# Who empties the turned keys: ScalarE alone with two buffers, or ScalarE and VectorE with three

## The reference, cut to what matters

```python
kv = (cond @ Wkv + bkv).reshape(1, -1, 2, H, hd)
k, v = (kv[:, :, 0], kv[:, :, 1])
q = _fq_sym(q, axis=-1)      # per head: max|x|/127, round, scale back
k = _fq_sym(k, axis=-1)
v = _fq_sym(v, axis=2)       # one scale per channel over all 4096 rows
attn = jnp.einsum('bhqd,bhkd->bhqk', q, k)
```

## Time and profile before

| what | value |
|---|---|
| time, median of 3 runs | 683.85 us (683.26 to 685.11) |
| the profiled execution | 682.87 us, span 681.1 us |
| granted TensorE clock, mean | 0.92 |
| `kv_stage`, first to last instruction | about 281.0 to 350.2 us |
| PE, DVE, ACT, POOL busy over the span | 86%, 72%, 59%, 49% |

### The profile page before, as it was taken

How to read it: one execution, slowest core, us unless ns; L and a number is a source line. 1 busy time by engine, 2 the same in 40 slices (tenths; PEclk the granted TensorE clock), 3 DMA queues, 4 the chain that set the end, 5 groups by cost and what they waited for, 6 DMA issues and landing times. The chain is left out here.

```text
span 681.1 us, 12859 instructions
## 1 busy us (share of the span) xinstructions
PE 587.4 (86%) x4813; PEld 398.3 (58%) x4813; DVE 493.7 (72%) x846; ACT 401.7 (59%) x754; POOL 335.9 (49%) x265
## 2 busy tenths in 40 slices
PE   4976899997899999788964988988888878889997
PEld 3542354444677776567740565655555465668886
DVE  4357999996677874567776999999999955433322
ACT  4226975552535544457875999999999953421111
POOL 1009999996204443243615889888888840000000
PEclk9987999999999999999975787779879869999999
DMA  8626600000936664035566889896979738900000
GB/s 336 254 74 252 247 0 1 0 1 0 303 119 212 211 218 130 16 115 147 150 167 149 162 129 183 152 168 136 165 159 149 132 64 326 408 2 1 0 1 15
DMA packets 97091, 92.90 MB, mean 136 GB/s; under 512 B 70596, under 2 KB 88324, under 8 KB 93639
## 3 DMA queue, kind: packets, MB, share of 16 engines
q1 hardware_dynamic: 84352, 85.74, 46.3%
q10 hardware_dynamic: 12678, 6.36, 3.2%
HBM read 68.59 MB, written 6.62 MB: 110 GB/s over the span
## 5 line engine op out<-in xcount | busy, mean ns | idle before, releaser
L2133 DVE TENSOR_REDUCE d_nmax<-d_psum 128x1 f32<-128x1024 f32 x128 | 152.0, 1214 | 6.0 <-PE d_psum L2289 6.0
L2289 PE MATMUL d_psum<-kst,qT 96*128 96x512 bf16 x256 | 97.2, 479 | 32.8 <-ACT d_e L2230 13.6
L528 POOL TENSOR_TENSOR b_h<-b_h,b_cb 128x1024 f32<-128x1024 f32 x32 | 88.0, 2750 | 6.5 <-DVE b_h L578 5.7
L2230 ACT ACTIVATE d_e<-d_psum,d_nmax 128x1024 f32<-128x1024 f32 x64 | 71.3, 1118 | 14.5 <-DVE d_nmax L2133 14.0
L2113 POOL TENSOR_SCALAR d_rounded<-d_e,d_lift 128x1024 f16<-128x1024 f32 x64 | 72.8, 1137 | 13.0 <-issue 7.0
L2113 POOL TENSOR_SCALAR d_rounded<-spare,d_lift 128x1024 f16<-128x1024 f32 x62 | 70.2, 1133 | 16.9 <-ACT d_lift L2234 12.6
L578 DVE TENSOR_TENSOR_SCAN b_h<-b_dA,b_psum 128x1024 f32<-128x1024 f32 x32 | 73.1, 2286 | 2.5 <-ACT b_dA L633 2.0
L633 ACT ACTIVATE b_dA<-b_dtT,b_A 128x248 f32<-128x248 f32 x128 | 53.7, 490 | 33.1 <-DVE b_h L578 28.1
L2230 ACT ACTIVATE spare<-d_psum,d_nmax 128x1024 f32<-128x1024 f32 x64 | 71.4, 1121 | 1.9 <-DVE d_nmax L2133 1.9
L2316 PEld LDWEIGHTS d_psum<-d_ident_f,d_rounded 128*128 128x128 f16 x512 | 44.1, 120 | 32.8 <-issue 20.9
L689 PE MATMUL b_psum<-b_bdiag,b_dtx 128*128 128x512 f32 x128 | 60.2, 594 | 0.8 <-DVE b_h L578 0.8
(11 more groups left out here) (439 smaller groups left out, 1185.5 us busy)
## 6 DMA issues: line engine op xcount, KB each, us to landing
c_w<-in_w0gu SPq DMA_DIRECT2D x16, 768.0 KB, 4.8
kst<-kT_scratch SPq DMA_DIRECT2D x84, 128.0 KB, 2.7
w<-in_w SPq DMA_DIRECT2D x5, 1920.0 KB, 21.0
b_cb<-c_scratch SPq DMA_DIRECT2D x4, 2048.0 KB, 6.9
c_w<-in_w0dn SPq DMA_DIRECT2D x16, 384.0 KB, 5.7
kT_scratch<-k_kT ACTq DMA_DIRECT2D x15, 384.0 KB, 2.7
a_ctx<-in_ctx SPq DMA_DIRECT2D x2, 2048.0 KB, 19.8
k_ctxT<-in_ctxT SPq DMA_DIRECT2D x12, 256.0 KB, 3.0
```

The costliest lines, as they stand in the source:

```text
L528: nc.gpsimd.tensor_tensor(hv, hv, cv, ALU.mult).then_inc(hc_ready, 1)
L2133: nc.vector.tensor_reduce(nm[:, t, m:m + 1, f:f + 1], quarter(m, j).unsqueeze(1), AX.X, ALU.max, negate=True).then_inc(nm_ready, 1)
L2230: nc.scalar.activation(e[j].unsqueeze(1), quarter(m, j).unsqueeze(1), ACT.Exp, bias=nm[:, t, m:m + 1, f], accum_out=zp[:, t, m:m + 1, f]). ...
L2289: last = nc.tensor.matmul(quarter(m, j)[:, b * 512:(b + 1) * 512], qT[0:QROWS, m:m + 1, t * P:(t + 1) * P], kst[m % 2][0:QROWS, at:at + 51 ...
```

## The change

ScalarE keeps the first turned step of each iteration and now copies it at the head of its iteration, ahead of `copy_values` and `split0`. VectorE copies the second turned step of the iterations that have two (steps 2, 4, 7, 9), directly behind `quantize_keys`, and steps 14 and 15 as before. There are three alternating `kT` buffers and the one for the last step. The stores of steps 0 to 11 are issued by SyncE between its context loads, those of steps 12 to 15 by ScalarE. Two semaphores, one for each copying engine, replace `kT_ready`. The maxima of the values are cut otherwise: iteration 4 takes 2 steps, 7 takes 3, and 8, 9 and 10 take 1 each (before: iterations 3, 5, 7 and 9, 2 steps each).

```diff
-VALUES_MAX = {3: (5, 7), 5: (7, 9), 7: (9, 11), 9: (11, 13)}
+VALUES_MAX = {4: (5, 7), 7: (7, 10), 8: (10, 11), 9: (11, 12), 10: (12, 13)}
+BY_VECTOR = tuple(turned[1] for turned in TURNS if len(turned) == 2) + (14, 15)
+BY_SCALAR = tuple(m for m in range(16) if m not in BY_VECTOR)
+KT_SLOTS = 3
...
-        kT = [sb(f"k_kT{s}", [P, K_PARTS * KC, KEYS], BF16) for s in range(2)] + [g["kT_last"]]
+        kT = [sb(f"k_kT{s}", [P, K_PARTS * KC, KEYS], BF16) for s in range(KT_SLOTS)] + [g["kT_last"]]
...
+        def wait_copied(eng, m):
+
+            copied, own = (kT_by_vector, BY_VECTOR) if m in BY_VECTOR else (kT_by_scalar, BY_SCALAR)
+            eng.wait_ge(copied, own.index(m) + 1)
+
+        def store(queue, m):
+            wait_copied(queue, m)
+            queue.dma_start(g["kT_store"][:, :, m * KEYS:(m + 1) * KEYS], kT[slot(m)][:, :, :]).then_inc(kT_stored[slot(m)], 16)
+
+        def wait_slot(eng, m):
+
+            if KT_SLOTS <= m < LAST:
+                eng.wait_ge(kT_stored[m % KT_SLOTS], m // KT_SLOTS * 16)
...
-                for m in range(FIRST + CTX_SLOTS - 1, STEPS):
-                    if m >= FIRST + CTX_SLOTS:
-                        sp.wait_ge(v_psum, nth(m - CTX_SLOTS))
-                    load_context(sp, d, g, m)
-                for s in range(2):
-                    sp.wait_ge(kT_stored[s], EARLY_STEPS // 2 * 16)
+                for i in range(STEPS - FIRST):
+                    m = FIRST + CTX_SLOTS - 1 + i
+                    if m < STEPS:
+                        if i:
+                            sp.wait_ge(v_psum, i)
+                        load_context(sp, d, g, m)
+                    for turned in TURNS[i]:
+                        if turned < EARLY_STEPS:
+                            store(sp, turned)
+                for s in range(KT_SLOTS):
+                    sp.wait_ge(kT_stored[s], EARLY_STEPS // KT_SLOTS * 16)
...
                     quantize_keys(FIRST + i)
+                    for m in TURNS[i][1:]:
+                        copy_turned(m)
                     queries(i)
...
                 for i in range(STEPS - FIRST):
+                    for m in TURNS[i][0:1]:
+                        copy_turned(m)
                     if i:
                         copy_values(FIRST + i - 1)
                     split0(FIRST + i)
-                    for m in TURNS[i][0:1]:
-                        copy_turned(m)
                     split1(FIRST + i)
-                    for m in TURNS[i][1:]:
-                        copy_turned(m)
                     for m in TURNS[i]:
-                        store(m)
+                        if m >= EARLY_STEPS:
+                            store(act, m)
...
                     if m >= 2:
-                        pe.wait_ge(kT_ready, m - 1)
+                        wait_copied(pe, m - 2)
```

More of the change, by code:

```diff
@@ L1524, in layer1_memory @@
     g["qs"] = sb("qs", [P, TC, H, 100], BF16)
-    g["kT_stored"] = [sem(f"kT_stored{s}") for s in range(3)]
+    g["kT_stored"] = [sem(f"kT_stored{s}") for s in range(KT_SLOTS + 1)]
     g["w_inT"] = sb("w_inT", [P, KC, 2 * INNER])
@@ L1674, in kv_stage @@
         kT_psum = sem("k_kT_psum")
-        kT_ready = sem("k_kT_ready")
+        kT_by_scalar = sem("k_kT_by_scalar")
+        kT_by_vector = sem("k_kT_by_vector")
         kT_stored = g["kT_stored"]
@@ L1687, in slot @@
         def slot(m):
-            return 2 if m == LAST else m % 2
+            return KT_SLOTS if m == LAST else m % KT_SLOTS
+        def wait_copied(eng, m):
[7 more added lines that the diff above has]
+                eng.wait_ge(kT_stored[m % KT_SLOTS], m // KT_SLOTS * 16)
         psT = [ps[:, 4 + 2 * s:6 + 2 * s, :].rearrange("p a b -> p (a b)").bitcast(BF16)[:, 0:K_PARTS * KC * KEYS]
@@ L1769, in copy_turned @@
                     dve.wait_ge(kT_psum, m + 1)
[L1770 to L1773, removed]
+                    wait_slot(dve, m)
+                    nc.vector.tensor_copy(kT[slot(m)][:, :, :], psT[m % 2]).then_inc(kT_by_vector, 1)
                 for i in range(STEPS - FIRST):
@@ L1824, in copy_turned @@
                     act.wait_ge(kT_psum, m + 1)
[L1825 to L1831, removed]
+                    wait_slot(act, m)
+                    nc.scalar.activation(kT[slot(m)][:, :, :], psT[m % 2], ACT.Copy).then_inc(kT_by_scalar, 1)
                 def split0(m):
@@ L1875, in _ @@
                 keep_queries(0)
-                store(LAST - 1)
+                store(act, LAST - 1)
                 keep_queries(1)
-                store(LAST)
+                store(act, LAST)
                 act.wait_ge(v_copied, nth(LAST))
@@ L2055, in _ @@
                 last_keys(sp, g["kT_last"], kst[0], k_in[0], 0, range(TAKEN, len(PRODUCTS)))
-                sp.wait_ge(g["kT_stored"][0], STEPS // 2 * 16)
-                sp.wait_ge(g["kT_stored"][1], (STEPS // 2 - 1) * 16)
+                for s in range(KT_SLOTS):
+                    sp.wait_ge(g["kT_stored"][s], STEPS // KT_SLOTS * 16)
                 load_keys(sp, d, kst[0], k_in[0], 0, LATE, range(TAKEN, len(PRODUCTS)))
@@ L2060, in _ @@
                 last_keys(sp, g["kT_last"], kst[1], k_in[1], 1)
-                sp.wait_ge(g["kT_stored"][2], 16)
+                sp.wait_ge(g["kT_stored"][KT_SLOTS], 16)
                 for dst, name in ((wp, "wp"), (bp, "bp")):
@@ L2214, in _ @@
                 last_keys(act, g["kT_last"], kst[0], k_in[0], 0, range(TAKEN))
-                act.wait_ge(g["kT_stored"][0], STEPS // 2 * 16)
-                act.wait_ge(g["kT_stored"][1], (STEPS // 2 - 1) * 16)
+                for s in range(KT_SLOTS):
+                    act.wait_ge(g["kT_stored"][s], STEPS // KT_SLOTS * 16)
                 load_keys(act, d, kst[0], k_in[0], 0, LATE, range(TAKEN))
```

## The result

Twelve runs of the changed kernel have a median of 682.57 us, twelve of the kernel before 684.48; the ratio is 0.9946, with a 95% interval of 0.992 to 0.9973. In microseconds of 683.85 that is 3.7 won, interval 1.8 to 5.5, where 3.0 were forecast (680.85, range 679.0 to 682.7; 683.85 x 0.9946 = 680.2). A second measurement of the same kernel on the chip of the last experiments gave 0.9958, interval 0.9931 to 0.9984.

What follows compares the result with a forecast made beforehand. TensorE, stalled by ScalarE's copies, was taken to bind before, ScalarE from iteration 5 on after. Gain: 2.7 us at step 10, 0.0 beyond, 0.3 credit, 3.0 in all: 683.85 to 680.85 us, range 679.0 to 682.7.

Steps and rivals of the forecast that it cites:

- TensorE unhindered through iteration 5: TensorE's 5.3 us of waits for ScalarE's copies gone through iteration 5; iteration 6 starts near 311.5.
- The bound was ScalarE from iteration 5 on: Steps 10 to 15: ScalarE's five rounds, uncovered while GpSimd works, take 26.8 us where TensorE would want 24.5.
- `split0` of step 15 carries the end: Stage end: a fixed chain of 6.19 us follows this `split0`, so the stage gains only what step 15 gains there.
- 2.7 us won at step 10: Iteration 5: VectorE has step 10 quantized at 313.0, where `split0` of step 10 started at 315.71 before.
- Nothing won from step 10 to step 15, 27.8 against 27.9: ScalarE's rounds 26.8, plus 0.4 for GpSimd's query rest and 0.6 for shared-access holds: 27.8 us, against 27.9 traced.
- 0.3 credited for my walk's own error: The walk put through the kernel before ended 0.7 us later than the trace; half, 0.3, was added to the gain.
- Stores and third buffer at nothing: Stores moved to SyncE, third key buffer: both priced 0, as a store's issue holds ScalarE for nothing; stores' other bound 4.4 us.
- Copies not held by GpSimd: VectorE's four new copies from PSUM: taken as 0 held; copies as slow as 1.4 us would cost 2.3.
- Rival 2: VectorE late in iterations 4 to 6 by slow copies or held quantization: 2.3 of 3.0 us go, 683.1; chance 0.12.
- rival 1: ScalarE does not bind because its rounds are shorter: the whole 6.4 us stall goes, 677.5; chance 0.06.
- rival 3: VectorE's thicker work holds GpSimd in ScalarE's uncovered rounds: slower, 686 at 0.6 a piece, 689.6 at the extreme; chance 0.06.
- Rival 4: The gain does not pass the barrier; the next stage's opening, with late keys, takes it back: 683.9; chance 0.06.

Runs made afterwards that it cites:

- the last experiments: Changed kernel with ScalarE's copy under the GpSimd round in iteration 10, or iterations 7 to 10, and VectorE's last two maxima moved: ratios to before 0.9921 and 0.9943.
- experiment 5: Changed kernel with ScalarE's first query part done twice in iteration 5 (2.03 us put in): stage 68.37 us against 65.93, 2.44 longer.
- experiments 1: Changed kernel with ScalarE making all copies, the second of an iteration behind `split1`, VectorE only steps 14 and 15: stage 72.70 us against 65.93.

## Why the prediction was right, step by step

- **TensorE unhindered through iteration 5.** Right, nearly to the digit: iteration 6 was forecast at 311.5 and starts at 313.02, which by before's start of the stage (1.52 earlier) is 311.50.
- **The bound was ScalarE from iteration 5 on.** Right: behind `split0` of step 10 its row has no gap but the rounds' waits for GpSimd, and experiment 5 gives back all of what it adds. That `split0` of step 15 carries the end was right too: 6.19 us behind it before, 6.22 after.
- **2.7 us won at step 10.** Too high: 34.54 - 32.57 = 1.97. VectorE quantized step 10 at 313.0 in my sum; by the same start it was 313.7. I had 0.3 for what GpSimd holds up; the trace has this:

```profile
311.00 1.16 POOL L1827 TENSOR_TENSOR k_parts<-k_rest,k_parts 128x512 bf16<-128x512 f32 x1 [0.74 <-ACT k_parts L1859]
...
311.08 1.36 DVE L1788 TENSOR_TENSOR v_own_max<-v_own_max,k_v_step_max 128x256 f32<-128x256 f32 x1
```

  GpSimd started 0.08 us ahead, and the 0.43 addition took 1.36, the same 0.93 as in the earlier trace rows.
- **Nothing won from step 10 to step 15, 27.8 against 27.9.** It took 27.14, so 0.8 were won. The five rounds by the rows were 26.8; of the 1.0 that I added, 0.3 came in sum. The 0.4 for GpSimd's rest of the queries was right (0.17 and 0.33 beyond 1.27). The 0.6 for holds did not come, and the third query part, which is shorter, took 1.53 where I had 1.78. The sum at step 15 is 2.74: the 0.7 lost at step 10 and the 0.8 won behind it cancelled. That the total came out near the forecast is luck to this extent; each half was off by 0.7 or 0.8, the whole by 0.3.
- **0.3 credited for my walk's own error.** The profiles say 2.71 in two of two executions, so the credit was not there. The time's ratio says 3.7, with 2.7 inside its interval.
- **Stores and third buffer at nothing.** Wrong as prices of the parts, though not in the sum: the sum was made of rounds that had no pair of stores in them and took the buffers as given. Taken back singly they cost 2.05 and 3.24 us. The step that failed is "an issue holds ScalarE for nothing": its rows showed one store, and with the copies made by VectorE two stand together, which hold ScalarE for 0.96 us where `split1` alone takes 0.54.
- **Copies not held by GpSimd.** The five copies of the alternating buffers took 949 ns on average. The four in the loop met GpSimd for at most 0.1 us, so whether one would be held is still not shown. Rival 2's mechanism was there in size (holds of 0.93 and 0.98) and in part in effect: the first is most of the 0.7 lost at step 10, and TensorE waited 0.4 for a copy.
- **The other rivals.** TensorE's whole 6.4 us did not come back (rival 1). GpSimd's subtractions kept 1.16 to 1.18 on average, the same as before, and one took 1.34; rival 3 did not occur. The stage's gain passed the barrier: VectorE's first maximum of the attention starts 2.16 us behind the last copy, 350.78 against 348.62, as before (351.96 against 349.81, 2.15). Rival 4 fails there; behind that point the profiles scatter by more than the gain.

## What to carry to other kernels

When a wait for a copy is cured by moving it to the head of the copying engine's iteration, look at what it used to cover there: here the order itself won 0.0 us and the second engine's copies carried the change, though without the stores' move they would have won 0.7 (68.64 - 67.98). Price the parts of a change also by taking each back out of the finished kernel; stores and buffers that look free beside the old order cost 2.0 and 3.2 us when only they were missing. Such prices depend on each other and do not add up: the copies' 6.8, the buffer's 3.2, the stores' 2.0 and the maxima's 0.5 are far more than the 2.7 of the whole. And follow the chain to the one instruction on which the end hangs: moving a single copy behind it in the last iteration won 1.3 us.

## What the runs showed that I had not expected

- Two stores in a row on ScalarE's queue leave it idle for 0.39 to 1.27 us; one behind `split1` leaves it none. One that has to wait for ScalarE's own copy costs 0.44 even alone, as the kernel before shows in iteration 5, where the query part stands behind it:

```profile
320.01 2.00 ACT L1855 ACTIVATE qs<-k_qq 128x1536 bf16<-128x1536 f32 x1 [0.44 <-ACT k_kT L1827]
```

- Two long waits cost TensorE more than their own length. Behind waits of 3.23 and 2.12 us its granted clock was 0.50 for a while (experiments 1 and 5); in the changed kernel, whose longest wait up to 345 us is 1.5, it was 1.00 from 285 to 347.5 us.
- Stores of 384 KB land later from SyncE, where they share the queue with context loads: the median from issue to landing is 3.7 us against 2.7 from ScalarE. Whether the loads are the cause is not shown.
- VectorE's two-input products are held as well: the one of the queries, 0.68 before, took 1.66 in the changed kernel while GpSimd subtracted:

```profile
315.97 1.16 POOL L1824 TENSOR_TENSOR k_rest<-k_kq,k_parts 128x512 f32<-128x512 f32 x1 [3.81 <-ACT k_parts L1855]
...
316.01 1.66 DVE L1782 TENSOR_TENSOR k_qq<-k_qi,k_q_scale 128x512 f32<-128x512 int16 x1
```

  The Trainium skill (Advanced Engine Details and Errata, VectorE Performance Modes) says that two-port instructions of VectorE and GpSimd's instructions block each other. The rows agree that one waits for the other, here for an instruction with two inputs in SBUF; whether it ran in a two-port mode, no run shows.

- The length of the stage repeats to 0.01 us from one execution to the next, while its start scatters over 4.9 us, with the same instructions ahead of it.
